# One branch on TensorE around all rounds in place of one in every round

## The reference

```python
x = _layernorm(x + attn(x))
wg, wu, wd = (w.astype(x.dtype) * (1.0 / 127.0) for w in (w_gate, w_up, w_down))   # 768x256, 768x256, 256x768
h = jax.nn.silu(einsum('bsd,hd->bsh', x, wg)) * einsum('bsd,hd->bsh', x, wu)
out = _layernorm(x + einsum('bsh,dh->bsd', h, wd))
```

## Time and profile before

| | us |
|---|---|
| median of 3 runs | 326.41 |
| the three runs | 324.96, 326.41, 333.9 |
| the profiled execution | 325.1 |
| its span, first to last instruction | 323.3 |
| TensorE busy in it | 280.9 (87%) |
| VectorE busy in it | 272.6 (84%) |
| ScalarE busy in it | 218.0 (67%) |
| GpSimd busy in it | 148.8 (46%) |

### The profile page before, as it was taken

How to read it: one execution, slowest core, us unless ns; L and a number is a source line. 1 busy time by engine, 2 the same in 40 slices (tenths; PEclk the granted TensorE clock), 3 DMA queues, 4 the chain that set the end, 5 groups by cost and what they waited for, 6 DMA issues and landing times.

```text
span 323.3 us, 4411 instructions
## 1 busy us (share of the span) xinstructions
PE 280.9 (87%) x1250; PEld 205.6 (64%) x1250; DVE 272.6 (84%) x484; ACT 218.0 (67%) x386; POOL 148.8 (46%) x123
## 2 busy tenths in 40 slices
PE   7878869908997999599997999999989998999892
PEld 5624756505885468465885568846785588868782
DVE  4999798629985999669986899899989998989664
ACT  3587767069764688529884498569855986299275
POOL 2564255491569019560378208570759056006030
PEclk9979799976997999989997999999999999999998
DMA  7802200402000301012010401020012001101002
GB/s 256 296 0 65 68 1 2 132 0 65 32 3 3 130 3 65 2 30 102 2 65 5 130 0 65 0 74 23 6 58 65 0 1 67 36 0 65 2 6 99
DMA packets 13531, 16.38 MB, mean 51 GB/s; under 512 B 704, under 2 KB 11200, under 8 KB 13504
## 3 DMA queue, kind: packets, MB, share of 16 engines
q1 hardware_dynamic: 12816, 15.48, 14.5%
q10 hardware_dynamic: 688, 0.53, 0.5%
HBM read 11.81 MB, written 4.19 MB: 50 GB/s over the span
## 4 chain that ended last, share of the span: by engine, by line
DVE 32%; PE 30%; issue 17%; ACT 15%; DMA 3%; DVEq 1%; POOL 1%; SPq 0%; ACTq 0%; POOLq 0%
PE bank_b L980 7%; PE bank_b L1012 6%; PE bank_a L1012 6%; DVE hid L758 4%; DVE wts L633 3%; ACT L512 3%; PE bank_c L970 3%; DVE stats L712 3%; DVE pmax L616 3%; DVE state L662 3%; ACT den L452 2%; ACT x L437 2%; ACT den L458 2%; DVE res L725 2%; DVE rwkv L705 2%
## 5 line engine op out<-in xcount | busy, mean ns | idle before, releaser
L348 POOL TENSOR_TENSOR hlo<-hid,hhi 128x512 fp32r<-128x512 f32 (+1 forms) x36 | 47.5, 1321 | 123.2 <-ACT hhi L496 123.2
L333 POOL TENSOR_TENSOR mix<-mix,xt 128x512 f32<-128x512 f32 x48 | 56.7, 1213 | 13.0 <-ACT mix L422 13.0
L1035 PE MATMUL bank_a<-wd_r,hhi 128*128 128x256 f32 x192 | 47.3, 287 | 4.6 <-DVE hlo L766 4.6
L422 ACT ACTIVATE mix<-dx,par 128x512 f32<-128x512 f32 x48 | 31.2, 710 | 27.0 <-POOL dx L327 26.9
L1035 PE MATMUL bank_a<-wd_r,hlo 128*128 128x256 f32 x192 | 45.6, 279 | 0.0
L980 PE MATMUL bank_b<-woT,rwkv 128*128 128x256 f32 x128 | 34.9, 432 | 8.6 <-issue 7.6
L1035 PEld LDWEIGHTS bank_a<-wd_r,hhi 128*128 128x128 f32 x192 | 36.0, 188 | 7.8 <-issue 7.0
L496 ACT ACTIVATE hhi<-hid 128x512 fp32r<-128x512 f32 (+1 forms) x54 | 31.1, 578 | 10.6 <-DVE hid L758 10.6
L980 PEld LDWEIGHTS bank_b<-woT,rwkv 128*128 128x128 f32 x128 | 27.2, 218 | 14.7 <-issue 8.8
L1035 PEld LDWEIGHTS bank_a<-wd_r,hlo 128*128 128x128 f32 x192 | 36.0, 188 | 0.3 <-issue 0.2
L414 ACT ACTIVATE wts<-wts 128x512 f32<-128x512 f32 (+1 forms) x54 | 27.9, 578 | 8.3 <-DVE wts L633 8.3
(11 more groups left out here) (103 smaller groups left out, 571.7 us busy)
## 6 DMA issues: line engine op xcount, KB each, us to landing
xt<-xT SPq DMA_DIRECT2D x7, 513.0 KB, 4.7
xrow<-x SPq DMA_DIRECT2D x7, 512.0 KB, 3.8
out<-y SPq DMA_DIRECT2D x6, 512.0 KB, 2.8
wg_i<-wg SPq DMA_DIRECT2D x1, 768.0 KB, 7.7
wu_i<-wu SPq DMA_DIRECT2D x1, 768.0 KB, 9.1
wd_i<-wd SPq DMA_DIRECT2D x1, 768.0 KB, 10.4
out<-y SPq DMA_DIRECT2D x3, 256.0 KB, 2.1
xt<-xT SPq DMA_DIRECT2D x2, 257.0 KB, 3.0
```

The lines of the kernel that those rows point to most:

```text
L333: nc.gpsimd.tensor_tensor(mix[:, s, i, h, 0:n], mix[:, s, i, h, 0:n], xt[:, h, 0:n], ALU.add).then_inc(mixed, 1)
L348: nc.gpsimd.tensor_tensor(hlo[:, m, 0:n], hid[:, m % NH, 0:n], hhi[:, m, 0:n].bitcast(f32), ALU.subtract).then_inc(hlo_ready, 1)
L422: nc.scalar.activation(mix[:, s, i, h, 0:n], dx[:, h, 0:n], ACT.Copy, scale=par[:, MIX + i, h:h + 1]).then_inc(dx_scaled, 1)
L1035: mm = nc.tensor.matmul(ffn[:, q, :], hp.bitcast(f32) if full else hp, w[:, m, :], start=(m == 0 and q % 2 == 0 and part is hhi), stop=(m ...
```

## The change

`round_` no longer branches; it gets the version as an argument. Rounds 1 to 8, the loop among them, and the last chunk's FFN products become one function `rounds(full)`, which is issued twice: once in the `If` with `full=False`, once in the `Else` with `full=True`. The loop exists twice in the program too. Nothing else of the kernel changes, and the programs of the other four engines are the same, row for row.

```diff
-            def round_(j, s, ffn, nxt):
+            def round_(j, s, ffn, nxt, full=False):
                 if ffn:
-                    with pe.If(any_wide == 0):
-                        ffn_products(j, False)
-                    with pe.Else():
-                        ffn_products(j, True)
+                    ffn_products(j, full)
...
-            round_(1, 0, True, True)
-            round_(2, 1, True, True)
-            with pe.Fori(3, NC - 2, 2) as j:
-                round_(j, 0, True, True)
-                round_(j + 1, 1, True, True)
-            round_(NC - 2, 0, True, True)
-            round_(NC - 1, 1, True, False)
+
+            def rounds(full):
+                round_(1, 0, True, True, full)
+                round_(2, 1, True, True, full)
+                with pe.Fori(3, NC - 2, 2) as j:
+                    round_(j, 0, True, True, full)
+                    round_(j + 1, 1, True, True, full)
+                round_(NC - 2, 0, True, True, full)
+                round_(NC - 1, 1, True, False, full)
+                ffn_products(NC, full)
+
             with pe.If(any_wide == 0):
-                ffn_products(NC, False)
+                rounds(False)
             with pe.Else():
-                ffn_products(NC, True)
+                rounds(True)
```

## The result

| | before | after |
|---|---|---|
| median of the runs first shown | 326.41 us (3 runs) | 315.44 us (4 runs, 314.61 to 316.15) |
| the profiled execution | 325.1 | 316.15 |
| its span | 323.3 | 314.4 |

The ratio is 0.9685, 95% interval 0.9629 to 0.974; two later comparisons gave 0.964 (0.9585 to 0.9696) and 0.9629 (0.9583 to 0.9675). The kernel is 3.2 to 3.7% faster. The ratios leave out executions more than 1.5% above a kernel's fastest, of which the kernel before has many (333.9 us here, 5 of 11 in the next comparison) and the changed kernel none. The kernel before had a fourth run of 458.12 us, which no comparison uses.

The account below looks back on a forecast made before the run. No engine bounds the 323.3 us span; the removable part was issue waits at long branches. 10.2 + 1.1 = 11.3 us gained, profiled execution 325.1 to 313.8, median 314.4 us, range 312.4 to 318.2.

Parts of the forecast that it names:

- The cause: Before the attention's output product, branches over the fp32 version wait 3.3 to 3.8 us for an instruction block not fetched ahead.
- Rounds 2, 3 and 4: Pauses before the output product and the slow clock behind them go: 10.2 us gained, priced by whole stretches.
- The FFN products of rounds 3 to 5: FFN products after the three disturbed stretches take a little longer once undisturbed: 0.3 us given back.
- the first rival: Clock stays low behind the output product for another cause; only 8.7 us gained, 316.4 to 317.7 us; 6%.
- Round 8: Long branch before the dummy products goes: 1.10 us on the chain gained.
- Short branches: Twelve short executions of the per-round branch, some 2 us together, hidden under queued products: gain 0.
- the compare at the top: The flag's compare now happens once, where the first one was: 0.
- straight code: TensorE's program crosses instruction block borders by running on, as before: cost 0.
- the loop's way back: The jump at the end of the loop's first pass, 255 ns before, with less code now: cost 0.
- The second: Rival: the loop's jump back misses and fetches, costing 0 to 3.3 us, up to 317.1 us; 5%.
- the fourth rival: Straight code reaches block borders before their fetches, 3.3 us each at about ten borders, some 347 us; 2%.
- The branch at the end: Long branch over the fp32 copy, 3.3 to 3.8 us, covered by the exit's wait for stores: cost 0.

Follow-up runs that it names:

- e3: Kernel before with all TensorE branches kept, each Else holding one dummy product in place of the fp32 version; 313.38 us, ratio 0.9601.
- e5: Changed kernel with the branch over the fp32 version put back in round 2 alone; 319.36 us, ratio 0.9768.
- e8: Kernel before with six dummy products ahead of the long branch in rounds 2 to 7; 328.56 us, ratio 1.0057.
- e2: Changed kernel without the fp32 version, so no branch but the loop's; 313.95 us, ratio 0.9622.
- e6: Kernel before with 256 never-run dummy products in the last chunk's Else, making the end's branch long; 327.76 us, ratio 1.000.

## Why the prediction was right or wrong

*The cause* was right, and is shown: with the same branches over a short distance the pauses are gone (e3), with one branch back over the long distance one pause is back (e5).

*Rounds 2, 3 and 4* were forecast at 10.2 us and gave 10.9. The method, whole stretches against undisturbed rounds, gave rounds 3 and 4 exactly (15.04 us). The FFN products of rounds 3 to 5 gave back 0.29 us together, for 0.3 forecast. The rest is round 2, which took 14.33 us: its transposes had nothing to wait for. That the lower clock belongs to the pause is shown by e8, so the first rival falls.

*Round 8*: 1.1 forecast, 1.3 measured.

*Short branches, the compare at the top, straight code, the loop's way back*: 0 each, and nothing speaks against it: e3, with all its short branches, was no slower than e2 with none. The way back at L1110 took 231 ns, and no pause stands inside FFN products. The second and the fourth rival fall. That q8 moved 10 packets where about 10 were forecast is luck: 7 came with the straight code up to 300 us, and 3 behind the branch at the end, which the forecast had not counted.

*The branch at the end* is the step that failed. It was priced at 0 because the exit waits for the stores until long after TensorE is through. The branch took 4.8 us in place of 3.3 to 3.8. That cover held even so (310.2 against 314.0 us), but the exit's wait itself grew, by 1.9 us in the profile, as the fetch took a transfer engine from the last store. I had priced the fetch as time of TensorE only, and never as traffic. Three profiles of the changed kernel show the store at 4.0, 3.1 and 4.5 us, and e5 and e6, which also end on a long branch, at 3.2 and 2.6; the nine profiles without one, the kernel before included, all at 2.1. That the two go together is shown; the price, between 0.5 and 2.4 us, is read from the landings. The medians put it at 0.95 us (e2) or 1.5 us (e3, which has more branches), and do not resolve it.

*The start* gave 1.1 us away in the profile. It is chance, as far as seen: two later profiles of the kernel before reach round 2's FFN products at 79.25 and 79.56 us, three of the changed kernel at 79.57, 79.08 and 79.28, and only the first profile of before at 78.48. The profile from which I summed had an early start.

*The size.* Forecast 11.3 us, 314.4 us in all. Over the spans it was 8.9, which is 12.3 gained in the rounds, 1.9 lost at the end, and 1.4 in what the two executions differ by anyway. The median, 315.44 us, is 1.0 us over the forecast. That it is no more is in part luck: profile against profile the miss is 316.15 - 313.8 = 2.4 us, and the changed kernel's profiled execution was its slowest of four. The chance of a fifth long branch in the kernel before, 4.4 us in its round, was in no term. The trace had the hint: round 7's branch was short (0.38 us) where those of rounds 2 and 8, written out like it, were long, and the prediction gave no reason.

## What to carry to other kernels

A branch costs by where it lands, not by being one: look up the longest execution of each branch's line, in more than one profile. Where it is some 3 us, put the two versions of the whole stretch apart rather than each piece in turn. Price a fetch of instructions twice, once on the engine that waits for it and once as a transfer beside whatever moves then, a kernel's last store above all. And a pause of 2.4 us in a busy TensorE costs more than itself, here 1.65 us of lower clock on top, part of which other waits may hide.

## What the runs showed of the hardware

- One 16 KB packet of instructions on one of 16 transfer engines went with a 256 KB store that landed 0.5 to 2.4 us later (2.6, 3.1, 3.2, 4.0 and 4.5 us from issue to landing, against 2.1), and with a 513 KB load that took 5.7 us, against 4.6 to 5.3 without.
- The same branch over the same code was short (0.38 us) in two executions of a program and long (3.51 us) in a third.
- TensorE ran the loop's second pass without a fetch: q8 moved nothing from 184.7 to 252.8 us in the kernel before, with the skipped versions between, and nothing from 175.8 to 243.2 us in the changed one.
- Multiplying zeros for 2.75 us while a fetch ran kept the granted clock of the next product at 1.00, where standing idle for 2.4 us led to 0.68 over the next 5.4 us.
